# Two window-attention blocks: three orders changed in the last slot of a group, and one transposed tensor moved to another bank

## Time and profile before

| | |
|---|---|
| median of 3 runs | 10272.33 us (10254.93 to 10277.12) |
| the profiled execution | 10271.18 us |
| its span, first to last instruction | 10268.8 us |
| PE busy | 8609.3 us (84%) |
| DVE, ACT, POOL busy | 6776.9 (66%), 6671.1 (65%), 4166.4 us (41%) |
| mean granted clock of PE | 0.903 |
| swin | from the start to about 5974 us |
| plain | from about 6157 us to the end |

### The profile page before, as it was taken

One profiled execution on the slowest core, in us unless ns is written; L12 is line 12 of the kernel. 1 busy time (PEld: TensorE's weight loads), 2 busy tenths in 40 slices (PEclk: granted clock), 3 DMA queues, 4 the chain that ended last, 5 costly groups with the idle time before them and its releaser, 6 DMA issues. The chain is left out here.

```text
span 10268.8 us, 317764 instructions
## 1 busy us (share of the span) xinstructions
PE 8609.3 (84%) x113246; PEld 6120.9 (60%) x113246; DVE 6776.9 (66%) x14138; ACT 6671.1 (65%) x12423; POOL 4166.4 (41%) x4662
## 2 busy tenths in 40 slices
PE   7888888888888888888888868888888888888888
PEld 4666666665666666666666646555555555655556
DVE  5777877777777777777787755555555545455544
ACT  5666766666666666666666656666666666666665
POOL 3544544444544544454454542222222222222222
PEclk9999999999988999999998979988999889899888
DMA  0000000000000000000000001111111111111111
GB/s 19 22 22 21 22 22 22 22 22 22 22 21 21 22 21 22 22 22 22 21 22 22 21 22 29 30 30 30 30 30 30 30 30 30 30 30 30 30 30 25
DMA packets 367885, 254.30 MB, mean 25 GB/s; under 512 B 271960, under 2 KB 347480, under 8 KB 366296
## 3 DMA queue, kind: packets, MB, share of 16 engines
q1 hardware_dynamic: 366298, 233.05, 8.9%
HBM read 78.66 MB, written 77.07 MB: 15 GB/s over the span
## 5 line engine op out<-in xcount | busy, mean ns | idle before, releaser
L755 POOL TENSOR_TENSOR swin_score<-swin_score,swin_top 113x588 f32<-113x588 f32 x1024 | 1203.1, 1175 | 2678.3 <-DVE swin_top L678 2675.7
L598 ACT ACTIVATE swin_probT<-ps_probs 128x339 f32<-128x339 f32 x2048 | 911.7, 445 | 1541.1 <-PE ps_probs L476 1540.8
L1177 ACT ACTIVATE plain_probT<-ps_probs 128x384 f32<-128x384 f32 x784 | 384.4, 490 | 1475.6 <-PE ps_probs L1104 1475.6
L476 PE MATMUL ps_probs<-swin_ident,swin_prob 113*128 113x113 f32 x6144 | 995.8, 272 | 69.8 <-ACT swin_probT L598 69.3
L476 PEld LDWEIGHTS ps_probs<-swin_ident,swin_prob 113*128 113x128 f32 x6144 | 764.1, 147 | 284.8 <-ACT swin_probT L598 141.8
L676 DVE TENSOR_TENSOR swin_score<-ps_scores,swin_bias_tab 113x588 f32<-113x588 f32 x1024 | 781.2, 763 | 205.6 <-PE ps_scores L490 202.4
L678 DVE TENSOR_REDUCE swin_top<-swin_score 113x12 f32<-113x588 f32 x1024 | 784.2, 766 | 35.2
L524 PEld LDWEIGHTS ps_dense<-swin_w_fc,swin_hid 128*98 128x98 f32 x6144 | 669.6, 196 | 136.2 <-issue 135.2
L583 ACT ACTIVATE swin_prob<-swin_score 113x588 f32<-113x588 f32 x1024 | 714.1, 697 | 4.9 <-POOL swin_score L755 2.0
L524 PE MATMUL ps_dense<-swin_w_fc,swin_hid 128*98 128x96 f32 x6144 | 711.4, 281 | 0.7 <-ACT swin_hid L589 0.7
L1333 POOL TENSOR_TENSOR plain_var_eps<-plain_moments,plain_epsilon 128x4 f32<-128x4 f32 x196 | 38.9, 198 | 1626.6 <-DVE plain_moments L1269 1626.6
(11 more groups left out here) (184 smaller groups left out, 22767.9 us busy)
## 6 DMA issues: line engine op xcount, KB each, us to landing
swin_k_heads<-swin_k_hat SPq DMA_DIRECT2D x1024, 36.8 KB
plain_x_in<-between_blocks SPq DMA_DIRECT2D x784, 48.0 KB, 2.2
plain_k_heads<-plain_k_hat SPq DMA_DIRECT2D x392, 96.0 KB, 2.1
out_dram<-plain_x SPq DMA_DIRECT2D x784, 48.0 KB, 2.0
swin_x_in<-in_x SPq DMA_DIRECT2D x224, 136.5 KB
between_blocks<-swin_x SPq DMA_DIRECT2D x224, 136.5 KB
swin_x_in<-in_x SPq DMA_DIRECT2D x224, 19.5 KB
between_blocks<-swin_x SPq DMA_DIRECT2D x224, 19.5 KB
```

The source lines that it names most:

```text
L476: last = nc.tensor.transpose(psP[:, n * QT:(n + 1) * QT], prob[0:QT, ts, 2 * hp:2 * hp + 2, :].rearrange('p h k -> p (h k)'), ident[0:QT, ...
L598: nc.scalar.activation(to, psP[:, 0:3 * QT], ACT.Copy).then_inc(did['probT'], 1)
L755: nc.gpsimd.tensor_tensor(view, view, bcast(top[0:QT, half, :], 2, WIN), ALU.subtract).then_inc(did['shifted'], 1)
```

## The change

In swin, four orders change; no instruction is added or taken away.

- PE, slot 3: the second half of the exponentials is turned ahead of the squared norms instead of behind them.
- ACT, slot 3: the exponentials go behind the copy of turned exponentials and behind `x1T_high`.
- DVE, slot 3: `x1T_low` goes ahead of `sq_norm`, which stays one pass of DVE over both banks.
- DVE, slot 0: `z` is read ahead of `normalise`.

In plain, the MLP input is transposed into bank A instead of B. Its transposes wait for the last GELU of the MLP (`hid`), `xT` and the read of the projection (`proj_read`) instead of `k_read`, `v_heads` and `fc2_read`. The projection, also in bank A, now waits for `x1T_low`; the second MLP layer and the values, in bank B, wait for it no longer.

```diff
@@ swin, PE
+                        if slot == 3:
+                            turn_probs(*before(g, slot, 2), 1)
                         if slot == 3 and exists(turn, groups):
                             pe.wait_ge(did['qk_sq'], upto(turn))
...
                             last.then_inc(did['norms_made'], 1)
-                        turn_probs(*before(g, slot, 2), 1)
+                        if slot != 3:
+                            turn_probs(*before(g, slot, 2), 1)
@@ swin, ACT, slot 3
-                            exponentials(*before(g, slot, 1))
                             copy_turned(*before(g, slot, 2), 0)
...
                                 nc.scalar.activation(x1T_high[:, :], psM[0:DIM, A, 0:NT], ACT.Copy).then_inc(did['x1T'], 1)
+                            exponentials(*before(g, slot, 1))
@@ swin, DVE, slot 0
-                            normalise(*before(g, slot, 3))
...
                                 nc.vector.tensor_tensor(z[:, :, :], out_of, bcast(row_fc2[0:TT, :], 1, PAIRS), ALU.add).then_inc(did['fc2_read'], 1)
+                            normalise(*before(g, slot, 3))
@@ swin, DVE, slot 3
+                            if exists(out2, groups):
+                                dve.wait_ge(did['x1T'], upto(out2))
+                                nc.vector.tensor_tensor(x1T_low[:, :], psM[0:DIM, A, 0:NT], x1T_high[:, :].bitcast(F32), ALU.subtract).then_inc(did['x1T_low'], 1)
                             if exists(turn, groups):
...
                                 nc.vector.tensor_scalar(sq_norm[:, :, :], psM[0:DIM, B:C + 1, 0:NT], 1e-06, None, ALU.max).then_inc(did['sq_norm'], 1)
-                            if exists(out2, groups):
...
@@ plain, PE
                             pe.wait_ge(did['mixedT'], upto(out2, 1, 2))
+                            pe.wait_ge(did['x1T_low'], upto(mlp))
                             pe.wait_ge(did['hid'], upto(fin, 2, CHUNKS))
...
                             pe.wait_ge(did['x1_norm'], upto(out2))
-                            pe.wait_ge(did['k_read'], upto(turn))
-                            pe.wait_ge(did['v_heads'], upto(make))
-                            pe.wait_ge(did['fc2_read'], upto(fin))
+                            pe.wait_ge(did['hid'], upto(mlp, 2, CHUNKS))
+                            pe.wait_ge(did['xT'], upto(turn))
+                            pe.wait_ge(did['proj_read'], upto(out2))
                             for p in range(PAIRS):
-                                last = nc.tensor.transpose(psM[0:DIM, B, p * TT:(p + 1) * TT], x1_norm[:, p, :], ident[0:TT, 0:TT])
+                                last = nc.tensor.transpose(psM[0:DIM, A, p * TT:(p + 1) * TT], x1_norm[:, p, :], ident[0:TT, 0:TT])
...
                             pe.wait_ge(did['hid'], upto(fin, 2, CHUNKS))
-                            pe.wait_ge(did['x1T_low'], upto(mlp))
+                            pe.wait_ge(did['k_read'], upto(make))
+                            pe.wait_ge(did['v_heads'], upto(g))
                             pe.wait_ge(did['fc2_read'], upto(g - 5))
...
                             pe.wait_ge(did['k_read'], upto(make))
-                            pe.wait_ge(did['x1T_low'], upto(mlp))
```

More of the change, by code:

```diff
@@ L737, in body @@
                                 nc.vector.tensor_scalar(sq_norm[:, :, :], psM[0:DIM, B:C + 1, 0:NT], 1e-06, None, ALU.max).then_inc(did['sq_norm'], 1)
-                            if exists(out2, groups):
-                                dve.wait_ge(did['x1T'], upto(out2))
-                                nc.vector.tensor_tensor(x1T_low[:, :], psM[0:DIM, A, 0:NT], x1T_high[:, :].bitcast(F32), ALU.subtract).then_inc(did['x1T_low'], 1)
                 run_groups(dve, groups, 16, body)
@@ L1219, in body @@
                                 act.wait_ge(did['fc1_made'], upto(mlp, 2, CHUNKS))
-                                nc.scalar.activation(x1T_high[:, :], psM[0:DIM, B, 0:NT], ACT.Copy).then_inc(did['x1T'], 1)
+                                nc.scalar.activation(x1T_high[:, :], psM[0:DIM, A, 0:NT], ACT.Copy).then_inc(did['x1T'], 1)
                 run_groups(act, groups, 12, body)
@@ L1297, in body @@
                             dve.wait_ge(did['x1T'], upto(out2))
-                            nc.vector.tensor_tensor(x1T_low[:, :], psM[0:DIM, B, 0:NT], x1T_high[:, :].bitcast(F32), ALU.subtract).then_inc(did['x1T_low'], 1)
+                            nc.vector.tensor_tensor(x1T_low[:, :], psM[0:DIM, A, 0:NT], x1T_high[:, :].bitcast(F32), ALU.subtract).then_inc(did['x1T_low'], 1)
                 run_groups(dve, groups, 12, body)
```

## The result

The changed kernel takes 10035.35 us, the median of 4 runs (10029.12 to 10040.03); the kernel before took 10267.28 us on the same chip. The ratio is 0.9774, with a 95% interval of 0.9757 to 0.9791. The forecast was 9944 us, with 9800 to 10200 as the range.

| | before | after | measured | predicted |
|---|---|---|---|---|
| swin, first to last norms | 5898 us | 5470 us | -428 | -360 |
| plain, first to last transposes of `x1_norm` | 4088 us | 4289 us | +201 | +33 |
| PE's mean granted clock | 0.903 | 0.905 | | |

A forecast was written before the change was run, and what follows sets the result against it. DVE's queue to `x1T_low` was taken to bound swin ahead of the projection, PE's falling clock second. From 10271.18 us, swin's -360 and plain's +33 gave 9944 us, range 9800 to 10200.

The forecast's parts named there:

- Swin's queue and waits: Swin slots 3 and 0: `x1T_low` 0.88 us earlier, full-clock group 21.68 to 20.80 us, PE waits 1.34 and 1.05 us.
- `z` at nothing: Swin slot 0, DVE: `z` ahead of `normalise` costs between 0 and 0.1 us, taken as 0.
- The price of zero for the turned exponentials: Swin slot 3, PE and ACT: scores end 0.3 us later, exponentials 0.9 us later, costing nothing at full clock.
- Swin's clock: Swin: falls follow the 2.22 us wait, now halved; one group in three falls at 2.2 us, mean 21.53 us.
- the price of the clock: Plain: the clock still falls, later, on the projection and what follows; with the work, +0.17 us x 196 = +33 us.
- again about 1.6 us: Plain: the later fall, on the projection and what follows it, costs about as much as the old fall.
- the bounds -1.2 to +0.35: Plain, per group: -1.2 us if the fall costs nothing more, +0.35 us as the change's cost without the clock.
- What the prediction said to look for: Plain: no wait ahead of `x1_norm` transposes, one ahead of the projection, regular groups 20.4 to 20.9 us, clock 0.85 to 0.92.
- rival 1: Swin's clock falls as often and dearly as now, only the 0.88 us gained: 10107 us; chance 0.18.
- Rival 2: Swin: the longer wait ahead of the norms costs the clock in nearly every group, 3.1 us: 10510 us; chance 0.10.
- Rival 3: Plain keeps its 1.2 us a group, -235 us instead of +33: 9676 us; chance 0.12.
- Rival 4: Swin: the projection waits for something else as late, time stays at 10270 us; chance 0.05 with smaller mixtures.

The follow-up runs named there:

- no_z: Swin half of the change alone, but with `normalise` left ahead of `z` on DVE, plain as before: 9839.56 us, ratio 0.9578.
- turned_first: Swin half of the change without the exchange of `x1T_low` and `sq_norm` on DVE, plain as before: 10279.1 us.
- fill_swin_before: Kernel before, no order changed, plus 14 needless transposes in swin's 2.22 us wait ahead of the projection: 10287.34 us.
- low_first: Kernel before with one edit only, `x1T_low` ahead of `sq_norm` on DVE in swin's slot 3: 9879.56 us.
- fill_swin_two: Kernel before plus needless transposes in two swin waits, 14 ahead of the projection and 6 ahead of the norms: 9949.48 us, ratio 0.9689.
- fill_both: Changed swin with 8 needless transposes in its 1.36 us wait, old plain with 17 in its 2.57 us wait: 9420.54 us, ratio 0.9169.
- fill_plain_before: Changed swin, plain as before with 17 needless transposes in its 2.57 us wait: 9583.94 us.

## Why the prediction was right, and where it was not

**Swin's queue and waits: right to a few hundredths.** DVE bound PE ahead of the projection. The exchange moved it by 0.87 us (21.68 to 20.81; 0.88 predicted), and the two waits came out at 1.36 and 1.02 us. `z` at nothing: shown by no_z. The price of zero for the turned exponentials: turned_first has the old period of 21.70 us.

**Swin's clock: the right size from slightly wrong parts.** I had one group in three at 2.2 us. It is three of 15 at 2.1 us (after, 4168.02:4190.92 and its like), less than I had feared; the turn of the loop stayed at 26.36 where I had 26.4. In the stretch that gives 344.8 us against 349.4, and over swin -428 against -360. The reason that I gave, that the long wait is what falls follow, holds only in part: fill_swin_before takes the long wait away and the falls move to the 1.02 us one. low_first, too, leaves both places, and brings the two waits down from 3.24 to 2.36 us together. Their sum is not the explanation either: in a full-clock group of fill_swin_before they are 1.02 and 0.43 us, and its swin spends 1079 us at half clock, that of before 1007. low_first and the changed kernel differ from it in the period of a group as well (20.81 against 21.69 us). Why the falls became rarer in swin stays open: no run tells the lengths of the waits, their distance and the period apart.

**Plain: the step that failed is the price of the clock.** The sum had +0.35 us for the work at full clock and "again about 1.6 us" for the fall, less what the first fall had cost, and took +0.17 us a group from the bounds -1.2 to +0.35. Measured are +0.13 at full clock (19.18 against 19.05) and +1.03 in all (201 / 196), outside the upper bound. The smaller part of the sum was mis-sized too: the old fall was taken at 1.6 us and measures 1.43 (20.48 - 19.05), which brings +0.35 down to +0.18, near the +0.13. (The 1.74 us read for the projection at half clock is of the group with the turn; in regular groups after it is 1.59 to 1.88.) The upper bound assumed that a fall costs afterwards what it costs before. Before, it came with the transposes of `x1_norm` and the exponentials and was over before the projection in every regular group. After the change it comes later, with the projection both in the regular groups and in those of 24.80 us. What differs is how long it lasts: 3.3 us at half clock cost 1.55 us, 6.8 and 7.0 us cost 2.19 and 2.70, and 13.9 us cost 5.62, since the clock then stays low through the whole second MLP layer. Before, 3.3 us cost 1.43. So a group loses 0.3 to 0.5 us for each us at half clock, before and after alike. It is the length of the falls that the sum had wrong. That they last longer because they now begin ahead of the long run of 24 matmuls is a guess that no run tests, and in 5 of 12 groups a fall at the same place is short. What the prediction said to look for (no wait ahead of the transposes, a wait ahead of the projection, regular groups of 20.4 to 20.9 us at 0.92) is all there, in those 5 groups. I never asked what the other groups could cost.

The ceiling should have been worked out as in swin, from a long fall. For swin I did that (2.57 to 3.45), for plain I did not, though the kernel before had such a group behind each turn of the loop. It loses 23.30 - 19.05 = 4.25 us:

```profile
8045.76:8069.06 23.30, 20.14 (x207) 0.79 0.12 27
```

**What was luck.** The total is only 91 us from the forecast because two errors offset each other: swin gained 68 us more than the sum had and plain lost 168 more.

**The rivals.** The time of 10035 us lies between the forecast and rival 1 (10107), but not by rival 1's cause: swin's clock did rise. The excess comes from plain. Rival 2 (the longer first wait decides) is refuted in the changed kernel, yet fill_swin_before shows its mechanism at work, at a wait of 1.02 us. Rival 3 (plain keeps its 1.2 us) is refuted: plain lost 1.03 us a group, and even at full clock it gains nothing (+0.13). Rival 4 is refuted by the timeline.

## What to carry to other kernels

Where PE's clock falls in steady groups, work out two periods: the one at full clock, from queues and waits, and the price of a fall, for a short one and for the longest that the trace holds. Moving or splitting a wait can move the fall and change how long it lasts: plain's one wait of 2.57 us became four of 2.24 us together, and the time at half clock rose from 857 to 1355 us. Before any reordering for the clock's sake, put needless transposes into all of PE's waits: that tells in one run what the clock costs. Here, with swin's new orders kept, they were worth 420 us (9840.79 to 9420.54), more than the whole change (232).

## What the runs showed of the hardware

- The clock fell to half in steady groups without a wait longer than 1.02 us: in fill_swin_before that is the longest idle time of a group, once in 21.7 us, the next are 0.43 and 0.24, and L567 takes 2.93 us behind it instead of 1.56. With that wait filled as well (fill_swin_two) nearly all groups keep the full clock. The Trainium skill says on the page "TensorE: Matmul & The Clock Gate", section "A second HAM failure mode: psum-queue depth-cycling", that short idles of PE between groups of matmuls, frequent enough, make the clock go up and down; this run agrees in kind.
- Extra matmuls in PE's waits made a kernel 4.3% faster (9840.79 to 9420.54 us, swin's new orders in both), and outside a wait slower. The same 14 transposes take 1.75 us at full clock and 2.96 when the clock has fallen just before.
- A group of plain loses 0.3 to 0.5 us for each us at half clock, whichever of six kinds it is (1.43 us for 3.3, 1.55 for 3.3, 2.19 for 6.8, 2.70 for 7.0, 4.25 for 9.8, 5.62 for 13.9).
- At a turn of the loop the clock still falls in the filled kernels (0.87 in fill_both, 0.82 in fill_plain_before). The turns were not filled; what filling them gives was not tried.
- The period of groups with a fall repeats closely: 20.47 to 20.50 us before, in ten groups of twelve, and 24.80 us in both dear groups of the twelve after and in the next one. Within a run the falls repeat in a pattern.
